# Message stages of a graph network: single groups against pairs of groups on TensorE

## The reference

```
fs = (h @ W).reshape(N_NODES, H, D)              # 4 heads of 64
alpha = softmax of leaky_relu(el[src] + er[dst]) over the edges of one dst
msg = alpha[:, :, None] * fs[src_e]
rst = jax.ops.segment_sum(msg, dst_e, num_segments=N_NODES)
h = (rst + b).sum(axis=1)                        # next step's h
```

## Time and profile before

| what | us |
| --- | --- |
| median of 3 runs | 2749.0 |
| lowest and highest | 2748.97 and 2749.05 |
| the profiled execution | 2749.61 |
| its span, first to last instruction | 2747.8 |

### The profile page before, as it was taken

The page is one execution under the profiler, slowest core; times in us unless marked ns, Lnnn a source line. Parts: engine busy times, 40 slices in busy tenths (PEclk is TensorE's granted clock), DMA queues, the critical chain, the costliest instruction groups (busy, mean ns, idle before and its releaser), DMA issues. The chain is left out here.

```text
span 2747.8 us, 39380 instructions
## 1 busy us (share of the span) xinstructions
PE 1924.2 (70%) x11482; PEld 1443.7 (53%) x11482; DVE 2025.3 (74%) x3688; ACT 1147.0 (42%) x2352; POOL 1796.8 (65%) x1700
## 2 busy tenths in 40 slices
PE   2655445479899759899749989849989991111685
PEld 2554434357566447666437766527756661000685
DVE  5776676677688477688567678768978887777697
ACT  0433333234333134343114433213346667665586
POOL 6777777657577736577736577746767764777333
PEclk9676666689877569887659967759989995555898
DMA  3444444211356201255301145412333331222574
GB/s 71 129 131 114 115 106 112 80 34 60 83 135 148 34 19 62 67 143 142 64 12 61 62 114 140 103 18 84 105 87 85 86 75 42 70 77 76 178 237 155
DMA packets 336364, 255.34 MB, mean 93 GB/s; under 512 B 175756, under 2 KB 284617, under 8 KB 336132
## 3 DMA queue, kind: packets, MB, share of 16 engines
q1 hardware_dynamic: 287876, 202.20, 24.9%
q0 software_dynamic: 43904, 48.80, 9.9%
q10 hardware_dynamic: 4372, 1.82, 0.3%
HBM read 132.21 MB, written 124.48 MB: 93 GB/s over the span
## 5 line engine op out<-in xcount | busy, mean ns | idle before, releaser
L1095 POOL DMA_INDIRECT edge<-table,row_of_source x588 | 557.2, 948 | 219.9 <-issue 171.9
L927 POOL TENSOR_TENSOR scaled<-edge 128x512 f32<-128x512 f32 x196 | 338.3, 1727 | 249.8 <-PE banks L1025 129.1
L981 DVE TENSOR_TENSOR_SCAN wide<-keep,wide,banks 64x256 f32<-64x256 uint8 x392 | 291.8, 744 | 129.6 <-PE banks L1033 115.1
L1004 ACT ACTIVATE scaled_t<-banks 128x1024 f32<-128x1024 f32 x196 | 200.7, 1024 | 318.3 <-PE banks L1025 318.3
L1234 ACT ACTIVATE wide<-h_new 64x512 f32<-64x512 f32 x147 | 92.6, 630 | 440.0 <-DVE h_new L1181 437.6
L1143 PEld LDWEIGHTS banks<-w_edge_full,wide 128*128 128x128 f32 x1176 | 209.1, 267 | 111.3 <-issue 99.2
L1575 POOL DMA_INDIRECT node_rows<-rows_conv,scatter_row x196 | 200.9, 1025 | 93.1 <-issue 56.0
L1136 PE MATMUL banks<-wide,w_row 128*64 128x512 f32 x294 | 229.6, 877 | 30.8 <-DVE h_new L1181 20.2
L1143 PE MATMUL banks<-w_edge_full,wide 128*128 128x72 f32 x1176 | 217.5, 348 | 47.9 <-DVE self_logit L1191 47.9
L202 POOL DMA_INDIRECT edge<-in_x_dram,src_row x196 | 193.5, 987 | 68.3 <-issue 57.9
L202 POOL DMA_INDIRECT got<-in_x_dram,dst_row x196 | 193.4, 987 | 59.7 <-issue 59.4
(11 more groups left out here) (297 smaller groups left out, 4426.4 us busy)
## 6 DMA issues: line engine op xcount, KB each, us to landing
node_rows<-x_out SPq DMA_DIRECT2D x97, 256.0 KB, 3.2
wide<-node_rows SPq DMA_DIRECT2D x48, 512.0 KB, 4.0
table<-chain_rows SPq DMA_DIRECT2D x147, 136.0 KB, 2.2
table<-rows SPq DMA_DIRECT2D x147, 136.0 KB, 2.3
nodes<-in_x_dram SPq DMA_DIRECT2D x97, 128.0 KB, 3.0
table<-x_out SPq DMA_DIRECT2D x97, 128.0 KB, 2.4
out_dram<-n_soft SPq DMA_DIRECT2D x48, 256.0 KB, 2.3
sources<-src_pad SPq DMA_DIRECT2D x49, 196.0 KB
```

Of the source, the lines that this page charges most:

```text
L927: pool.tensor_tensor(scaled[:, s, SHARE:], edge[:, mine, 0:D].unsqueeze(2).broadcast_to([P, TPG - SHARE, H, D]), inner(edge[:, mine, D:ROW ...
L981: v.tensor_tensor_scan(out=wide[0:D, bass.ds(first + 1, HALF_E)], data0=keep[:, s, half * HALF_E:(half + 1) * HALF_E], data1=bank[2 + s][h ...
L1004: s_.activation(scaled_t[:, s], banks[:, 6 * s:6 * s + 2], ACT.Copy).then_inc(taken, 1)
L1095: pool.indirect_dma_start(out=edge[:, at_tile], out_offset=None, in_=tables[l], in_offset=bass.IndirectOffsetOnAxis(ap=row_of_source[:, at ...
```

## The change

Groups go in turns: [0], [1, 2], [3, 4], up to [47, 48], 25 turns for 49 groups. `in_turns(fn, ks)` calls a stage's function for each group of a turn. The functions themselves stay as they were, but for two waits that are dropped on PE. T no longer waits for `taken` of k-2, and M no longer for `summed` of k-2; with the new order both hold already when these instructions come up. POOL's block is not touched.

```diff
+                turns = [[0]] + [[k, k + 1] for k in range(1, G, 2)]
+                def in_turns(fn, ks):
+                    for k in ks:
+                        fn(k, k, k % 2, k // 2)
@@ sync
-                    pipelined(sp, ((1, load), (1, load_x), (5, save)), lead=5)
+                    for i, ks in enumerate(turns):
+                        in_turns(load, ks)
+                        in_turns(load_x, ks)
+                        if i > 0:
+                            in_turns(save, turns[i - 1])
+                    in_turns(save, turns[-1])
@@ vector
-                    pipelined(v, ((0, scale), (3, scan)) + (((5, stage),) if last_step else ()), lead=5)
+                    in_turns(scale, turns[0])
+                    for i, ks in enumerate(turns):
+                        if i + 1 < len(turns):
+                            in_turns(scale, turns[i + 1])
+                        if last_step and i > 0:
+                            in_turns(stage, turns[i - 1])
+                        in_turns(scan, ks)
+                    if last_step:
+                        in_turns(stage, turns[-1])
@@ scalar
-                    pipelined(s_, ((1, take),) + (() if last_step else ((4, stage),)), lead=5)
+                    for i, ks in enumerate(turns):
+                        in_turns(take, ks)
+                        if not last_step and i > 0:
+                            in_turns(stage, turns[i - 1])
+                    if not last_step:
+                        in_turns(stage, turns[-1])
@@ tensor, transpose and message
-                        t_.wait_ge(taken, at(k, back=2))
-                        t_.wait_ge(summed, at(k, back=2))
@@ tensor
-                    pipelined(t_, ((1, transpose), (4, next_rows), (2, message)), lead=5)
+                    for i, ks in enumerate(turns):
+                        in_turns(transpose, ks)
+                        if i > 0:
+                            in_turns(next_rows, turns[i - 1])
+                        in_turns(message, ks)
+                    in_turns(next_rows, turns[-1])
```

## The result

| | before | changed |
| --- | --- | --- |
| median of 9 runs, us | 2749.11 | 2754.67 |
| lowest and highest | 2748.9, 2752.5 | 2752.17, 2760.88 |
| the profiled execution, its span | 2749.61, 2747.8 | 2759.19, 2757.4 |

The ratio is 1.0018, 95% interval 1.0009 to 1.0026. The forecast was 2751 in a range of 2740 to 2762. A second comparison, on another occasion, gave 1.0014 (1.0005 to 1.0023). So the kernel became slower: by 4.9 and 3.9 us by the ratios, by 5.6 and 4.7 us by the medians. That is clear of zero, and no more than about the 0.2% (5.5 us) that was set as the bound of no change.

A forecast was written before the change was run, and what follows sets the result against it. PE was taken to bound the message stages of steps 0 to 2. Their -8.6 us and step 3's +10.9 sum to +2.3, which against the median of 2749.0 gives 2751.3, say 2751; range 2740 to 2762.

The forecast's parts named there:

- The turn of 5.51 us: PE, steps 0 to 2: two groups take 5.51 instead of 5.76 us, -6.0 a stage (0 to -7.2).
- The margin of the second R: Steps 0 to 2: scans need 3.2 us after the first M, PE has 3.6 in between; holds by 0.4.
- The start: Each message stage's start: PE idles 1.15 us for group 0; clock rises 3.1 us later, losing 1.6 (0 to 3.3).
- The sum of steps 0 to 2: Each message stage: -6.0 + 1.15 + 1.6 + 0.4 = -2.85 us; three times -8.6.
- The two waits: Semaphore waits dropped on PE, long been met: put at nothing.
- Step 3: Last message stage: chain through the x load takes 12.1 us for four groups; stage +10.9 us (+5 to +15).
- The term of the x load: Last message stage: x load to POOL's add 2.59 us; mean excess 0.2 gives +2.4 (0 to 5) over twelve rounds.
- The total: Whole kernel: -8.6 + 10.9 = +2.3 us, 2751; within 0.50, slower than 2754.5 0.31, faster than 2743.5 0.19.
- The covered load: Last message stage: x load covered after all, stage gains 2.85 us; total -11.4, 2737.6; chance 0.18.
- No saving by pairs: PE's blocks pay the drain by their waits, not their kind; pairs save nothing, 2769 us; chance 0.07.
- a clock that falls under sixteen transposes: PE: transposes don't hold the clock up, a T block a turn at 1.2 GHz; +180 us, 2930; chance 0.02.
- A dearer chain: Last message stage: loads land 0.3 us later (+3.6) or add takes 1.28 us (+6.6); 2755 to 2761; chance 0.17.

The follow-up runs named there:

- M in full width: M as two products onto 128 partitions instead of four onto 64, half the message columns uncomputed: kernel before, period 2.63 us; changed kernel, turn 5.35 us.
- pairs from group 0: Changed kernel with x loads ahead of mask loads and turns [0, 1] to [46, 47], then [48]: 2730.33 against 2750.59 us, ratio 0.9926.
- the x loads first: Changed kernel with SP issuing a turn's two x loads ahead of its two mask loads: 2733.64 against 2749.13 us, ratio 0.9942; earlier run 0.9955.

## Why the prediction was right, and where it was off

- **The turn of 5.51 us.** Right to the digit. The two runs with M in full width bear out the reading that was given: PE loses 0.10 us at each of the two passages to and from M's 64-column blocks in a period, 0.25 with the 0.05 between T and R. That PE drains at a passage is not shown by itself.
- **The margin of the second R.** This reading was wrong. It was to hold by 0.4 us, but that compares the end of the first R with the end of the sum. The second R's first weight load starts before the first R's last record ends, and only 0.10 us after the sum in the trace. It needs some 0.05, so the margin is 0.05 us. It was luck that this cost only two turns of 5.8 us in each of steps 1 and 2.
- **The start.** Idle 1.15 us forecast, 1.11 measured. The clock was to rise 3.1 us later; it rose 8.9, 7.7 and 6.4 us after the first T in steps 0, 1 and 2, against 5.1, 4.9 and 4.8: later by 3.8, 2.8 and 1.6 us. That the rise hangs on the pause fits the ranges above, but its moment varies by 3 us within one order.
- **The sum of steps 0 to 2.** -2.85 each forecast, -2.9, -2.7 and -3.3 measured. More than half of what is missing from the saving of 6.0 is held back at the start: with pairs from group 0 and the x loads first, the four stages are 1.7 us shorter on the mean than with the x loads first alone, although a single group then stands at the end.
- **The two waits.** Nothing forecast, nothing that shows in the runs.
- **Step 3.** The chain is there as described: SP's order, POOL's add, scale(k) behind add(k-3), the second T of a turn. Put at 12.1 us for four groups plus 0.2 for late loads, it took 12.55 (3.137 a group). The term of the x load was too small: 2.59 us and a mean excess of 0.2 had been taken, the mean is 2.88 us. The 2.59 was a single row; the mean of the kernel before was already 2.90. The rest is 0.12 us from scale to T and 0.10 from T to the sum, by the table above. Against this, four groups took 11.62 us before and not 11.5, by the one late T. With all of it +10.9 became +12.6 (+11.6 in the second profile). The step was named for every second turn; the list shows T late in 16 turns of 24.
- **The total.** +2.3 forecast; +3.6 and +2.6 by the stages, 5.6 and 4.7 by the medians. The parts are those that were forecast, so it was not luck in them; but about half of the way from 2751 to 2754.67 is the rest outside the message stages, of which the prediction knew nothing. The median lies just above 2754.5, where the prediction had drawn the line to slower, with a chance of 0.31.
- **Rivals.** The covered load (2737) did not come, but the kernel with the x loads first is just that case and took 2733.64. No saving by pairs, and a clock that falls under sixteen transposes, are refuted by the turn of 5.51 and the clock of 1.00 in the second window above, which answers the earlier trace rows. A dearer chain, the third, is the side on which the result lies, though with less than the 2755 to 2761 given for it. Neither of its reasons came: the add took 0.73 us in the chain, and the x load landed in 2.70 us on the mean, against 2.66 before.

## What to carry to other kernels

An order by larger blocks is worth what the passages between blocks cost, and that can be read from the ends of blocks in one period before anything is changed. What margin is left to the next block is read to the start of its first weight load, not to the end of the block ahead. Every other engine's order must then be read again, above all the queue that issues transfers: when two loads with waits of different age are grouped, the one that could go early stands behind the one that can't. Here two lines in the other order turned a loss of some 5 us into a gain of 15.

## What was not expected of the hardware

- The same program took 2749 us on one chip and 3298 on another. In the two kernels that were profiled on both, message stages are equal within 1.1 us, while 359 to 370 us lie between two of them instead of 285 to 286. A gather between them takes POOL 0.95 us on either chip; what grows is POOL's idle time ahead of the gathers, from 220 to 435 us with the x loads first.
- A 128 KB load issued 0.56 us behind a 32 KB one landed in 2.7 us on the mean; issued 1.08 us behind it, in 2.3 (one profile, 20 loads). A delay at the issue was thus mostly given back at the landing.
- Four products of M onto alternating halves of 64 columns made the period of T, R and M 0.25 us longer than two onto 128 columns (2.88 against 2.63 us), though M's block spans 1.08 us either way. Most of that lies in the two passages to and from M's block, 0.10 us at each.
